# Perceiver block on one core: the output projection of the cross-attention moved around the key sums, the value product behind the next scores, 32 columns streamed in the sums, and the first pair's steps in another order

## The chip, the core and the metric

The kernel runs on one NeuronCore of a Trainium2 chip. Its engines are TensorE (PE, matmuls; its weight loads are shown apart as PEld), VectorE (DVE), ScalarE (ACT), GpSimd (POOL) and SyncE (SP), which issues nearly all DMAs here. Each engine takes its own list of instructions in order and waits on semaphores. The metric is the time of one execution on the device in microseconds (us); lower is better.

## The reference

A block of three parts, each added to x (512 tokens of 512 values, kept in fp32). In short:

```
x = x + cross_attention(layernorm(x), ctx)   # 8 batches: 64 queries, 256 keys; 16 heads of 128
x = x + chunked_linear_attention(layernorm(x))
x = x + moe(layernorm(x))                    # 32 experts, top 6, and a shared one

# cross_attention, per head h
q = rmsnorm(x @ Wq[h]) * gq ;  k = rmsnorm(ctx @ Wk[h]) * gk ;  v = ctx @ Wv[h]
out += softmax(q @ k.T / sqrt(128)) @ v @ Wo[h]
```

The change lies in the cross-attention alone.

## The kernel before

**Precision.** Most products are made of three passes on operands split into a high and a low part (`mm3`, lines 319 to 321): ACT copies the high part, DVE or POOL subtracts it to get the low part, and PE runs high x high, high x low, low x high. The sums of squares, the scores and the product with the probabilities are plain fp32.

**Pairs of heads.** The cross-attention takes heads two at a time, in HP = 8 pairs. `pair(0)` is written out, pairs 1 to 6 are the bodies of a hardware loop (`Fori`), and `last_pair` is written out again. A pair i works one stage ahead: while it makes its own softmax, it projects queries and keys for pair i+1, and it projects the output of pair i-1 (called y in the code) to x. On PE a body of the loop is: scores of pair i in four parts (`xa_pe_scores`, L724, two batches a part), queries of pair i+1 (`xa_pe_q`), its keys in eight parts (`xa_pe_keys`), the sums of squares of its keys and queries (`xa_pe_ss`, L707 and L711), the output projection of pair i-1 in four tiles of 128 tokens (`xo_pe`, `xo_pe_tile`), a transpose of the reciprocal norms (`xa_pe_rkT`, L717), then for each part the transposes of the probabilities (`xa_pe_pT`, L735) and their product with the context (`xa_pe_u`, L748), and last the product with the value weights (`xa_pe_ao`), which needs all four parts of u split in two.

**The sums.** A sum over the 128 partitions is a matmul with the squares as weights. `xa_pe_ss` loads 32 columns of squares as weights, streams one column of ones through them, and writes one PSUM column on 32 partitions; four such matmuls fill the 128. There are 128 for the keys and 32 for the queries in each pair, and each fp32 matmul stands as two instructions in the trace.

**Who feeds whom.** DVE multiplies scores with the keys' reciprocal norms `rkB` (L639), takes the maximum (L642) and scales it (L644); ACT takes the exponential (L606); DVE normalises (L649, L651). DVE copies the keys out of PSUM (L581), ACT squares them (`xa_act_ksq`, L576). After the sums come ACT's square root (`xa_act_rms`, L656), DVE's reciprocal (`xa_dve_rq`, L660), the transpose on PE, DVE's copy (L585), and on SP a store to DRAM and a broadcast load into `rkB`, for the next pair's scores. `xo_act_heads` and `xo_dve_heads` (L402, L407) split the result of `xa_pe_ao`; both stand at the end of a pair. `xo_dve` adds the four tiles of the projection to x (L444).

**Banks.** PSUM has eight banks of 512 fp32. `SB` gives the banks of the four score parts, `KB` those of the eight key parts, `SSB` that of the sums, `YB` and `YL` those of the projection's tiles. u takes banks 4 and 5, ao 6 and 7, the queries 2 and 3.

**The order** on each engine is the order of the calls in the code; nothing is scheduled. The first pair's keys, the first layer norm (`ln_*`) and the first queries stand ahead of `pair(0)` on every engine.

Of the kernel before, what the change touches and what calls it, by code (L numbers as in the profile page):

```python
# [38 lines left out]
def perceiver_block(nc, x_in, ctx_in, ctxT_in, Wq, Wk, WkT, Wv, Wo, gq, gk,  # L39
# [17 lines left out]
    with stack:  # L57
# [327 lines left out]
        SB = (4, 5, 0, 1)  # L385
# [29 lines left out]
        def xo_pe(e, i, last=False):  # L415

            e.wait_ge(wo_ready, i * 2 + 2)
            e.wait_ge(ao_split, i * 2 + 2)
            for t in range(TT):
                if last and t >= 2:  # L420
                    e.wait_ge(s_ready, (i + 1) * 4 + t + 1)
                if not last and t < 2:
                    e.wait_ge(kT_ready, (i + 2) * NK + (4 + t + 1))
                if not last and t >= 2:
                    e.wait_ge(qn_ready, (i + 2) * 2 + (t - 1))
                xo_pe_tile(i, t, YL[t] if last else YB[t])
# [124 lines left out]
        KB = (6, 7, 4, 5, 0, 1, 6, 7)  # L551
# [101 lines left out]

        def xa_act_rms(e, p):
# [42 lines left out]
        def xa_pe_ss(e, p):  # L697

# [3 lines left out]
            for n in range(NK):  # L702
                for s in range(4):
                    col = B + n % 2 * KT + n // 2 * 4 + s
                    for r in range(4):
                        at = s % 2 * P + r * Q4
                        m = e.matmul(ps[r * Q4:(r + 1) * Q4, SSB, col:col + 1], ksq(n)[:, s // 2, at:at + Q4],  # L707
                                     ones[:, 0:1], start=True, stop=True)
            for b in range(B):
                for r in range(4):  # L710
                    m = e.matmul(ps[r * Q4:(r + 1) * Q4, SSB, b:b + 1],  # L711
                                 sq[:, b, r // 2, r % 2 * Q4:(r % 2 + 1) * Q4], ones[:, 0:1], start=True, stop=True)
            m.then_inc(ss_ps, 1)

        def xa_pe_rkT(e, p, bank):
            e.wait_ge(soft_step, p * SOFT + 1)
# [580 lines left out]
        soft_step, rms_ready = sem("soft_step"), sem("rms_ready")  # L1297
# [238 lines left out]
        def _(e):  # L1536
# [8 lines left out]
            ctxT_hi(0)  # L1545
            ctxT_hi(1)
            for n in range(NK):
                xa_act_ksq(e, 0, n)
                if n in (1, 3):
                    ctxT_hi(2 + n // 2)  # L1550
                if n == 5:
                    ln_act_std(e, 0, 0, TT)
            xa_act_wq(e, 0)
            for t in range(TT):
                ln_tile_hi(e, 0, t)
            e.wait_ge(small_dve, DV_GQK)
# [3 lines left out]
            xa_act_rms(e, 0)  # L1560
            xa_act_wk(e, 1)

            def pair(i, more=True):
                xa_act_exp(e, i, 0)
                xa_act_wv(e, i)
                xa_act_exp(e, i, 1)
# [19 lines left out]
                xo_act_heads(e, i)  # L1586
            pair(0)
            with e.Fori(1, HP - 2) as i:
                pair(i)
            pair(HP - 2, False)  # L1590

            def last_pair(i):
                xa_act_exp(e, i, 0)
                xa_act_wv(e, i)
                for j in range(1, JB):
# [87 lines left out]
        def _(e):  # L1683
# [6 lines left out]
            ctxT_lo(0)  # L1690
            ctxT_lo(1)
            for n in range(NK):
                xa_dve_kT(e, 0, n)
                if n in (1, 3):
                    ctxT_lo(2 + n // 2)
                if n == 2:
                    e.wait_ge(x_in_s, 16)
                if n in (2, 3):
                    for t in range(2):
                        ln_stats(e, 2 * n - 4 + t)  # L1700
                if n == 4:
                    ln_mean_var(e)
            ln_tiles_inverse(e, 0, TT, 1)
            for t in range(TT):
                ln_tile_scale(e, t, xn_a)
            e.wait_ge(g_in_s, 32)
            e.tensor_tensor(gqk[:, 2:3], gqk[:, 0:1], gqk[:, 1:2], ALU.mult).then_inc(small_dve, 1)
            for t in range(TT):
                ln_tile_lo(e, 0, t)
# [518 lines left out]
```

## Time and profile before

| what | value |
|---|---|
| median of 3 runs | 1041.73 us (1037.94 to 1043.43) |
| the profiled execution: its own time, its span | 1042.17 us, 1040.4 us |
| mean granted TensorE clock | 0.962 of full |
| TensorE busy (share of the span) | 965.2 us (93%) |
| VectorE, ScalarE, GpSimd busy | 643.4 us (62%), 569.1 us (55%), 263.5 us (25%) |
| cross-attention | from the start to about 425 us |

The profile's span is the part between the first and the last recorded instruction; 1.8 us of the execution lie outside of it. A timeline row gives start, duration, engine, line, operation, output and inputs, and in square brackets how long the engine had idled before and who released it. A matmul's duration holds its way through the array; the cost of one in a dense row of them is the distance between starts. Consecutive instructions of one line are merged into a row with a count. "issue" as a releaser means that the profile shows nothing that was waited for.

### The profile page before, as it was taken

What the parts mean: (1) busy time and instruction counts of PE and PEld (TensorE: products, weight loads), DVE (VectorE), ACT (ScalarE), POOL (GpSimd) and SP (SyncE); (2) the same over time, 40 slices, a digit from 0 to 9 for tenths busy, and PEclk for the clock granted to TensorE, in tenths of its full rate; (3) what the DMA queues carried; (4) which work ended last, traced back from release to release, by engine and by line L of the source; (5) the groups of instructions that cost most, each with busy time, mean ns of one, the idle gap of its engine ahead of it and who ended that gap; (6) DMA issues with size and microseconds to landing.
All of it is one profiled execution on the core that took longest, in us unless ns stands there. A gap on an engine that the chain in (4) does not pass through costs nothing.

```text
span 1040.4 us, 23883 instructions
## 1 busy us (share of the span) xinstructions
PE 965.2 (93%) x8410; PEld 804.8 (77%) x8411; DVE 643.4 (62%) x1009; ACT 569.1 (55%) x925; POOL 263.5 (25%) x167
## 2 busy tenths in 40 slices
PE   7677889999999989989999999899999999999997
PEld 5556677777778778778888888777878889878885
DVE  5252535445352627667777777574848888778876
ACT  4353536446363637455555563444247888778773
POOL 0202202111111104133333330010023544545451
PEclk9897998989898989999999999999999999999999
DMA  4342320303031113422222200711348999998995
GB/s 161 113 113 72 133 72 30 91 10 102 3 99 33 39 41 84 152 82 81 81 81 81 71 30 25 246 40 41 117 161 291 283 318 323 361 340 273 308 347 173
DMA packets 74884, 143.07 MB, mean 138 GB/s; under 512 B 13556, under 2 KB 40564, under 8 KB 74592
## 3 DMA queue, kind: packets, MB, share of 16 engines
q1 hardware_dynamic: 66992, 130.43, 37.1%
q0 software_dynamic: 7856, 12.16, 5.1%
q8 instruction: 23, 0.38, 0.2%
q14 instruction: 13, 0.11, 0.0%
HBM read 144.76 MB, written 15.07 MB: 154 GB/s over the span
## 4 chain that ended last, share of the span: by engine, by line
PE 71%; DMA 8%; DVE 6%; SPq 5%; issue 5%; ACT 4%; DVEq 0%; ACTq 0%; POOLq 0%
PE ps L319 17%; PE ps L320 16%; PE ps L321 16%; PE ps L748 6%; PE ps L724 3%; DMA w_raw<-in_w 3%; SPq L1001 2%; PE ps L707 2%; PE ps L1034 2%; DMA wo_raw<-in_owT 1%; DMA y_scratch<-ob,give 1%; DMA w_and_lists<-in_w 1%; PE ps L1046 1%; SPq L1242 1%; PE ps L735 1%
## 5 line engine op out<-in xcount | busy, mean ns | idle before, releaser
L1059 DVE TENSOR_TENSOR w_l<-w_raw,w_h 128x1408 fp32r<-128x1408 f32 x76 | 121.8, 1624 | 32.7 <-ACT w_h L1055 24.9
L1055 ACT ACTIVATE w_h<-w_raw 128x1408 fp32r (+1 forms) x76 | 102.9, 1376 | 35.4 <-DMA w_raw<-in_w 32.9
L778 POOL TENSOR_TENSOR lw_l<-lw_raw,lw_h 128x1024 fp32r<-128x1024 f32 x32 | 77.3, 2432 | 133.8 <-ACT lw_h L774 128.9
L319 PE MATMUL ps<-w_h,xeT_h 128*128 128x352 f32 x288 | 97.4, 338 | 5.5 <-DVE w_l L1059 5.0
L320 PE MATMUL ps<-w_l,xeT_h 128*128 128x352 f32 x288 | 93.1, 323 | 0.0
L321 PE MATMUL ps<-w_h,xeT_l 128*128 128x352 f32 x288 | 92.9, 323 | 0.0
L1215 POOL DMA_INDIRECT xe<-xn_scratch,take x37 | 39.5, 1069 | 183.3 <-DVE give L1163 100.5
L1219 POOL DMA_INDIRECT y_scratch<-ob,give x34 | 80.2, 2357 | 22.5 <-issue 9.9
L319 PE MATMUL ps<-xT_hi,lw_h 128*128 128x512 f32 x192 | 78.2, 407 | 0.3
L321 PE MATMUL ps<-xT_hi,lw_l 128*128 128x512 f32 x192 | 76.4, 398 | 0.0
L320 PE MATMUL ps<-xT_lo,lw_h 128*128 128x512 f32 x192 | 76.1, 397 | 0.0
L748 PE MATMUL ps<-pT,ctx 128*128 128x128 f32 x512 | 63.7, 281 | 1.7 <-ACT pT L612 1.7
L581 DVE COPY kT<-ps 128x512 f32<-128x512 f32 x64 | 43.5, 688 | 33.1 <-PE ps L321 33.1
L748 PEld LDWEIGHTS ps<-pT,ctx 128*128 128x128 f32 x512 | 60.7, 196 | 3.6 <-ACT pT L612 3.6
L319 PEld LDWEIGHTS ps<-w_h,xeT_h 128*128 128x128 f32 x288 | 54.3, 189 | 10.1 <-DVE w_l L1059 10.1
L319 PE MATMUL ps<-cT_h,wk_h 128*128 128x512 f32 x128 | 51.9, 406 | 8.7 <-DVE cT_l L1687 5.1
L319 PE MATMUL ps<-wo_h,ao_h 128*128 128x512 f32 x128 | 57.0, 446 | 3.0 <-DVE ao_l L483 2.6
L397 POOL TENSOR_TENSOR wo_l<-wo_raw,wo_h 128x512 fp32r<-128x512 f32 x16 | 20.3, 1289 | 153.2 <-ACT wo_h L392 153.2
L665 DVE TENSOR_TENSOR u_l<-ps,u_h 128x512 fp32r<-128x512 f32 x32 | 22.1, 692 | 57.5 <-ACT u_h L617 57.5
L937 DVE RECIPROCAL q_r<-q_r 128x512 f32<-128x512 f32 x16 | 53.6, 3348 | 6.1 <-ACT q_r L913 6.1
L320 PE MATMUL ps<-wo_l,ao_h 128*128 128x512 f32 x128 | 54.8, 428 | 0.0
L321 PE MATMUL ps<-wo_h,ao_l 128*128 128x512 f32 x128 | 54.2, 423 | 0.0
(315 smaller groups left out, 2522.4 us busy)
## 6 DMA issues: line engine op xcount, KB each, us to landing
w_raw<-in_w SPq DMA_DIRECT2D x78, 704.0 KB
w_and_lists<-in_w SPq DMA_DIRECT2D x39, 512.0 KB
w_and_lists<-in_w SPq DMA_DIRECT2D x39, 192.0 KB
rkB<-rk_scratch SPq DMA_DIRECT2D x56, 128.0 KB, 3.1
wq_raw<-in_Wq SPq DMA_DIRECT2D x8, 512.0 KB, 5.1
wo_raw<-in_Wo SPq DMA_DIRECT2D x16, 256.0 KB, 2.7
lw_raw<-in_kwT SPq DMA_DIRECT2D x8, 512.0 KB, 3.3
lw_raw<-in_qwT SPq DMA_DIRECT2D x8, 512.0 KB, 3.4
```

What stands on the lines that cost most here:

```text
L319: nc.tensor.matmul(out_ap, lh, rh, start=first, stop=False)
L320: nc.tensor.matmul(out_ap, lh, rl, start=False, stop=False)
L321: return nc.tensor.matmul(out_ap, ll, rh, start=False, stop=last)
L581: e.tensor_copy(kT[:, n % 2, n // 2 * G4:(n // 2 + 1) * G4], ps[:, KB[n], :]).then_inc(kT_ready, 1)
L724: m = e.matmul(ps[k * SQ:(k + 1) * SQ, SB[j], n * SKV:(n + 1) * SKV], qn[:, k, b * SQ:(b + 1) * SQ], kT[:, k, kvb(b)], start=True, stop=True)
L748: m = e.matmul(ps[:, 4 + j % 2, at:at + P], ctx[:, b * KPB + t, hcol(c)], pT[:, b, t, :], start=t == 0, stop=t == KPB - 1)
L778: e.tensor_tensor(lw_l[n][:, :, :], lw_raw[n][:, :, :], lw_h[n][:, :, :], ALU.subtract).then_inc(lw_ready[n], 1)
L937: e.reciprocal(q_r[:, k, :], q_r[:, k, :]).then_inc(q_recip, 1)
L1055: e.activation(w13_h[:, k, n, :, :], w13_raw[:, slot(raw), n, :, :], ACT.Copy).then_inc(w13_hi_s, 1)
L1059: e.tensor_tensor(w13_l[:, k, n, :, :], w13_raw[:, slot(raw), n, :, :], w13_h[:, k, n, :, :], ALU.subtract).then_inc(w13_ready, 1)
L1215: e.indirect_dma_start(xe[:, k, :], None, xn_dram.ap(), bass.IndirectOffsetOnAxis(ap=take[:, k:k + 1], axis=0), bounds_check=T - 1, oob_is ...
L1219: e.indirect_dma_start(y_dram[k].ap(), bass.IndirectOffsetOnAxis(ap=give[:, k:k + 1], axis=0), ob[:, k, :], None, bounds_check=T - 1, oob_ ...
```

## The change

Seven edits, all within the cross-attention:

- `xo_pe` in the loop is split (`xo_pe_half`): tiles 0 and 1 now stand ahead of the sums, tiles 2 and 3 behind them. Tiles 0 and 1 wait for two of the key copies instead of for later ones. On DVE the additions of tiles 0 and 1 stand ahead of the reciprocal, and the others behind it.
- `xa_pe_ao` of pair i-1 stands in pair i, behind its four scores (in the last pair behind three of them). The splits `xo_act_heads` and `xo_dve_heads` go with it: on ACT behind the second exponential, on DVE behind the fourth scores. The copy of the value weights on ACT waits until ao has been made.
- The banks of scores are 0, 1, 4, 5 and those of key parts 2 to 5 are 0, 1, 4, 5, so that the first two scores don't touch u's banks. Scores 2 and 3 wait for the last two parts of u.
- The sums stream 32 columns of ones instead of one. Each matmul writes 32 PSUM columns, and the next of its rows overwrites all but the first; the queries' sums are made ahead of the keys', in order of columns.
- Ahead of pair 0 the keys' sums are made before the queries, and the queries' sums by themselves later, with their own square roots and reciprocals (`xa_act_first_rms`, `xa_dve_first_rk`, `xa_act_first_rms_q`, `xa_dve_first_rq`). The transpose of the keys' norms stands between the two query products.
- Ahead of pair 0, ACT makes all four high parts of the context before it squares keys, DVE three of the low parts before it copies keys; the copies, statistics and weight splits around them are reordered.
- The warm-up matmuls at the very start are 21 instead of 16.

```diff
-        SB = (4, 5, 0, 1)
+        SB = (0, 1, 4, 5)
-        KB = (6, 7, 4, 5, 0, 1, 6, 7)
+        KB = (6, 7, 0, 1, 4, 5, 6, 7)
...
+        def xo_pe_half(e, i, half):
+
+            e.wait_ge(wo_ready, i * 2 + 2)
+            e.wait_ge(ao_split, i * 2 + 2)
+            for t in (2 * half, 2 * half + 1):
+                if t < 2:
+                    e.wait_ge(kT_ready, (i + 2) * NK + (2 + t + 1))
+                else:
                     e.wait_ge(qn_ready, (i + 2) * 2 + (t - 1))
-                xo_pe_tile(i, t, YL[t] if last else YB[t])
+                xo_pe_tile(i, t, YB[t])
...
         def xa_act_wv(e, i):
             e.wait_ge(wv_in, i * 16 + 16)
+            if not isinstance(i, int) or i > 0:
+                e.wait_ge(ao_ps, i * 2)
...
+        def xa_pe_k_ss(e, p):
+            for k in range(2):
+                for t in range(KT):
+                    col = B + k * KT + t
                     for r in range(4):
-                        m = e.matmul(ps[r * Q4:(r + 1) * Q4, SSB, col:col + 1], ksq(n)[:, s // 2, at:at + Q4],
-                                     ones[:, 0:1], start=True, stop=True)
+                        at = t % 2 * P + r * Q4
+                        m = e.matmul(ps[r * Q4:(r + 1) * Q4, SSB, col:col + Q4], ksq(t // 4 * 2 + k)[:, t % 4 // 2, at:at + Q4],
+                                     ones[:, 0:Q4], start=True, stop=True)
...
         def xa_pe_u(e, i, j):
             e.wait_ge(pT_ready, i * 4 + (j + 1))
             if j < 2:
-                e.wait_ge(s_ready, i * 4 + (j + 1))
+                e.wait_ge(s_ready, i * 4 + (j + 3))
...
@@ ACT, pair @@
                 xa_act_exp(e, i, 0)
+                xa_act_exp(e, i, 1)
+                if y is not None:
+                    xo_act_heads(e, y)
                 xa_act_wv(e, i)
-                xa_act_exp(e, i, 1)
...
@@ DVE, pair @@
                 xa_dve_scores(e, i, 3)
+                if y is not None:
+                    xo_dve_heads(e, y)
                 xa_dve_norm(e, i, 2)
...
+                if y is not None:
+                    xo_dve_tile(e, y, 0, YB)
+                    xo_dve_tile(e, y, 1, YB)
                 xa_dve_rq(e, i + 1)
                 if y is not None:
-                    xo_dve(e, y)
+                    xo_dve_tile(e, y, 2, YB)
+                    xo_dve_tile(e, y, 3, YB)
...
@@ PE, ahead of pair 0 @@
+            e.wait_ge(kT_ready, NK)
+            e.wait_ge(ksq_ready, NK)
+            xa_pe_k_ss(e, 0).then_inc(first_ss, 1)
             e.wait_ge(xT_ready, TT)
             xa_pe_q(e, 0, 0)
+            xa_pe_rkT(e, 0, 6)
             xa_pe_q(e, 0, 1)
-            xa_pe_ss(e, 0)
+            e.wait_ge(sq_ready, 2)
+            xa_pe_q_ss(e).then_inc(ss_ps, 1)
@@ PE, pair @@
+                    if j >= 2 and y is not None:
+                        e.wait_ge(u_ready, y * 4 + (j + 1))
                     xa_pe_scores(e, i, j)
-                if isinstance(i, int) and i == 0:
-                    xa_pe_rkT(e, 0, 6)
+                if y is not None:
+                    xa_pe_ao(e, y)
                 xa_pe_q(e, i + 1, 0)
                 xa_pe_q(e, i + 1, 1)
                 xa_pe_keys(e, i)
+                if y is not None:
+                    xo_pe_half(e, y, 0)
                 xa_pe_ss(e, i + 1)
                 if y is not None:
-                    xo_pe(e, y)
+                    xo_pe_half(e, y, 1)
...
-                xa_pe_ao(e, i)
@@ PE, last pair @@
                 for j in range(JB):
+                    if j >= 2:
+                        e.wait_ge(u_ready, (i - 1) * 4 + (j + 1))
                     xa_pe_scores(e, i, j)
+                    if j == 2:
+                        e.wait_ge(u_ready, (i - 1) * 4 + 4)
+                        xa_pe_ao(e, i - 1)
                 xo_pe(e, i - 1, last=True)
```

**PE, the loop, at its seam.** The end of the loop's body before: transposes of the probabilities, their product with the context (L748), ao (`u_h,wv_h`), the jump back.

```order
L735 MATMUL ps<-ident,sc 128x128 x4
L748 MATMUL ps<-pT,ctx 128x128 x16
L319 MATMUL ps<-u_h,wv_h 128x512
L320 MATMUL ps<-u_l,wv_h 128x512
L321 MATMUL ps<-u_h,wv_l 128x512
```

And the start of the body in the changed kernel (L758 is the scores' line there, was L724; L2079 sets up the waits for u's splits), the end of which is now the product with the context:

```order
L758 MATMUL ps<-kT,qn 64x256 x8
L2079 ISA
L758 MATMUL ps<-kT,qn 64x256 x4
L2079 REGISTER_ALU
L758 MATMUL ps<-kT,qn 64x256 x4
L319 MATMUL ps<-u_h,wv_h 128x512
L320 MATMUL ps<-u_l,wv_h 128x512
L321 MATMUL ps<-u_h,wv_l 128x512
```

The twelve matmuls of ao have moved over the seam, behind the sixteen of the next scores, with the waits for u between the scores.

**PE, the loop, around the sums.** Before: the sums (weights from `lw_raw`, `ksq` and `sq`) follow on the last key part, and the projection (`wo_h,ao_h`) on them.

```order
L699 ISA
L700 REGISTER_ALU
L707 MATMUL ps<-ones,lw_raw 32x1 x16
L707 MATMUL ps<-ones,ksq 32x1 x16
L707 MATMUL ps<-ones,lw_raw 32x1 x16
L707 MATMUL ps<-ones,ksq 32x1 x16
L707 MATMUL ps<-ones,lw_raw 32x1 x16
L707 MATMUL ps<-ones,ksq 32x1 x16
L707 MATMUL ps<-ones,lw_raw 32x1 x16
L707 MATMUL ps<-ones,ksq 32x1 x16
L711 MATMUL ps<-ones,sq 32x1 x32
```

In the changed kernel, with the last rows of tile 1 ahead and the first of tile 2 behind:

```order
L320 MATMUL ps<-wo_l,ao_h 128x512
L321 MATMUL ps<-wo_h,ao_l 128x512
L723 ISA
L724 REGISTER_ALU
L742 MATMUL ps<-ones,sq 32x32 x32
L735 MATMUL ps<-ones,lw_raw 32x32 x64
L735 MATMUL ps<-ones,ksq 32x32 x64
L432 REGISTER_ALU
L319 MATMUL ps<-wo_h,ao_h 128x512
```

The count of sums is the same, 160; each streams 32 columns, and half the projection stands on either side.

**DVE, the loop, behind the fourth scores.** In the changed kernel the split of ao (L407) stands between the scaled maximum (L653, was L644) and the third normalisation; before, these rows stood at the end of the body.

```order
L653 TENSOR_TENSOR nmx<-nmx,rqk 128x2
L406 ISA
L407 TENSOR_TENSOR ao_l<-ps,ao_h 128x512
L406 REGISTER_ALU
L407 TENSOR_TENSOR ao_l<-ps,ao_h 128x512
L658 RECIPROCAL rsm<-sm 128x2
```

The first scores of a pair have nothing of ao ahead of them now; keys' parts 0 and 1, which reuse ao's banks, wait for these two rows.

## Rows read from the trace of the kernel before

**Rows 1.** Waits of PE from 0 to 400 us: total, times, longest.

```profile
PE ps L707 <- ACT ksq L576: 11.9, 7, 2.7
PE ps L319 <- DVE u_l L665: 10.5, 7, 1.5
PE ps L707 <- issue: 5.8, 3, 2.3
PE ps L319 <- DVE cT_l L1687: 5.1, 3, 2.2
PE ps L319 <- DVE xT_lo L374: 4.0, 1, 4.0
PE ps L711 <- issue: 3.4, 2, 1.9
PE ps L319 <- DVE sc L639: 3.2, 4, 1.6
```

**Rows 2.** Timeline of PE, pair 2, from its scores to the next pair's.

```profile
152.98 3.67 PE L724 MATMUL ps<-kT,qn 128*64 128x256 f32 x32
...
173.01 0.39 PE L320 MATMUL ps<-cT_l,wk_h 128*128 128x512 f32 x1
173.25 0.40 PE L321 MATMUL ps<-cT_h,wk_l 128*128 128x512 f32 x1
175.18 0.40 PE L707 MATMUL ps<-ones,lw_raw 128*32 128x1 f32 x29 [1.54 <-ACT ksq L576]
...
178.99 0.79 PE L319 MATMUL ps<-wo_h,ao_h 128*128 128x512 f32 x1
...
182.99 0.40 PE L319 MATMUL ps<-wo_h,ao_h 128*128 128x512 f32 x1
...
197.59 0.47 PE L319 MATMUL ps<-u_h,wv_h 128*128 128x512 f32 x1 [1.50 <-DVE u_l L665]
...
200.53 3.67 PE L724 MATMUL ps<-kT,qn 128*64 128x256 f32 x32
```

**Rows 3.** Windows: busy time of each engine, then granted clock, DMA share, GB/s.

```profile
177.00:179.00 2.00, 2.00 (x155) 1.99 (x147) 0.00 (x0) 0.80 (x1) 2.00 (x2) 0.50 0.00 0
183.00:185.00 2.00, 2.00 (x10) 1.67 (x9) 0.69 (x1) 0.00 (x0) 0.00 (x0) 1.00 0.00 0
```

**Rows 4.** Timeline of PE: sums before pair 0, and in pair 2.

```profile
40.89 0.43 PE L707 MATMUL ps<-ones,lw_raw 128*32 128x1 f32 x32 [0.69 <-ACT sq L593]
41.16 0.42 PE L707 MATMUL ps<-ones,ksq 128*32 128x1 f32 x31
...
177.16 0.60 PE L707 MATMUL ps<-ones,lw_raw 128*32 128x1 f32 x30
...
177.59 0.60 PE L707 MATMUL ps<-ones,ksq 128*32 128x1 f32 x30
```

**Rows 5.** Timeline of PE, second layer: 64 columns streamed, then one.

```profile
445.20 1.15 PE L817 MATMUL ps<-kq 128*64 128x64 f32 x32
446.18 1.05 PE L807 MATMUL ps<-ones,kq_sq 128*64 128x1 f32 x32
447.16 0.50 PE L319 MATMUL ps<-xT_hi,lw_h 128*128 128x512 f32 x1
```

**Rows 6.** Timeline of PE, pair 0: scores, sums and their end.

```profile
47.10 5.01 PE L724 MATMUL ps<-kT,qn 128*64 128x256 f32 x32 [0.39 <-ACT rms L656]
...
76.62 0.40 PE L707 MATMUL ps<-ones,lw_raw 128*32 128x1 f32 x29 [2.68 <-ACT ksq L576]
...
84.33 0.28 PE L711 MATMUL ps<-ones,sq 128*32 128x1 f32 x7 [1.85 <-issue]
```

**Rows 7.** Timeline of DVE, last pair: first scores, last scaled maximum.

```profile
392.42 0.68 DVE L639 TENSOR_TENSOR sc<-ps,rkB 128x512 f32<-128x512 f32 x1
...
400.03 0.16 DVE L644 TENSOR_TENSOR nmx<-nmx,rqk 128x2 f32<-128x2 f32 x1
```

**Rows 8.** Timeline of PE, last pair: its first transposes.

```profile
400.83 1.04 PE L735 MATMUL ps<-ident,sc 128*128 128x128 f32 x8
```

More of the change, by code:

```diff
@@ L420, in xo_pe @@
                 if last and t >= 2:
[L421 to L424, printed above, removed]
+                    e.wait_ge(s_ready, (i + 1) * 4 + t - 1)
+                xo_pe_tile(i, t, YL[t] if last else YB[t])
+        def xo_pe_half(e, i, half):
[5 more added lines that the diff above has]
+                else:
                     e.wait_ge(qn_ready, (i + 2) * 2 + (t - 1))
-                xo_pe_tile(i, t, YL[t] if last else YB[t])
+                xo_pe_tile(i, t, YB[t])
         def ao_half(n):
@@ L1544, in _ @@
             xa_act_wk(e, 0)
-            ctxT_hi(0)
-            ctxT_hi(1)
-            for n in range(NK):
+            for g in range(4):
+                ctxT_hi(g)
+            for n in range(4):
                 xa_act_ksq(e, 0, n)
[L1549 to L1552, printed above, removed]
             xa_act_wq(e, 0)
-            for t in range(TT):
+            for n in range(4, 6):
+                xa_act_ksq(e, 0, n)
+            ln_act_std(e, 0, 0, TT)
+            xa_act_ksq(e, 0, 6)
+            ln_tile_hi(e, 0, 0)
+            xa_act_ksq(e, 0, 7)
+            for t in range(1, TT):
                 ln_tile_hi(e, 0, t)
+            xa_act_first_rms(e)
+            xa_act_wk(e, 1)
             e.wait_ge(small_dve, DV_GQK)
@@ L1585, in pair @@
                 xo_act_weights(e, i)
-                xo_act_heads(e, i)
             pair(0)
             with e.Fori(1, HP - 2) as i:
-                pair(i)
-            pair(HP - 2, False)
+                pair(i, y=i - 1)
+            pair(HP - 2, False, HP - 3)
             def last_pair(i):
                 xa_act_exp(e, i, 0)
+                xa_act_exp(e, i, 1)
+                xo_act_heads(e, i - 1)
                 xa_act_wv(e, i)
-                for j in range(1, JB):
+                for j in range(2, JB):
                     xa_act_exp(e, i, j)
@@ L1689, in _ @@
             xa_wk_low(e, 0)
-            ctxT_lo(0)
-            ctxT_lo(1)
-            for n in range(NK):
-                xa_dve_kT(e, 0, n)
[L1694 to L1702, printed above, removed]
+            for g in range(3):
+                ctxT_lo(g)
+            xa_dve_kT(e, 0, 0)
+            xa_dve_kT(e, 0, 1)
+            ctxT_lo(3)
+            xa_dve_kT(e, 0, 2)
+            xa_dve_kT(e, 0, 3)
+            e.wait_ge(x_in_s, 16)
+            for t in range(TT):
+                ln_stats(e, t)
+            ln_mean_var(e)
+            for n in range(4, 7):
+                xa_dve_kT(e, 0, n)
             ln_tiles_inverse(e, 0, TT, 1)
@@ L1751, in last_pair @@
                 xa_dve_scores(e, i, 3)
+                xo_dve_heads(e, i - 1)
                 xa_dve_norm(e, i, 2)
@@ L2000, in _ @@
             e.wait_ge(consts, 2)
-            for _ in range(16):
+            for _ in range(21):
                 e.matmul(ps[:, 0, 0:P], ones[:, :], ones[:, :], start=True, stop=True)
```

50 lines of the change are left out of this document (33 added, 17 removed).

## The prediction

> **What bounds the kernel now.** I read the busy shares first: TensorE is busy 93% of the span, no other engine over 62%, so TensorE's list of work sets the time, and a gain must come from its idle stretches, from a higher clock, or from less work. The second view is the list of TensorE's waits up to 400 us, where the cross-attention lies [rows 1]. The reader is to see three kinds: 11.9 us for the squared keys ahead of the sums (7 times), 10.5 us for u's low part ahead of ao (7 times, 1.5 us each), and 9.2 us (5.8 and 3.4) of "issue" inside the sums, in five pieces, one of them in rows 6. Third, one pair of the loop in the timeline [rows 2]: it takes 200.53 - 152.98 = 47.55 us, and shows the two waits (1.54 and 1.50) and a stretch of projection matmuls that start 4.00 us apart for nine of them, where the keys' start 0.24 us apart. Fourth, the granted clock of windows [rows 3]: 0.50 of full in the sums and behind them (1.2 GHz), 1.00 (2.4 GHz) from 183 us. The engine's history before that fall is an idle stretch of 1.5 us and then matmuls that stream one column each. So a pair loses about 5 us that are not work, and the sums are slower than they could be.
>
> **The steady pair, term by term.** The change puts half the projection, 12 matmuls or 2.8 us, between the last keys and the sums. ACT's last square comes 1.5 us behind the keys, so the wait goes: the last key matmul starts at 173.25 and would be followed 0.24 later, the sums start at 175.18, so 1.69 us [rows 2]. Cover: 2.8 against 1.5 us. Behind the sums stand the other 12 matmuls, 2.8 us; square root, reciprocal and their hand-overs need about 1 us there, and were covered by all four tiles before. Ao, moved behind the next scores, has 16 scores (3.6 us) as cover for u's last split, whose wait is 1.50 us [rows 2]. Cover again suffices, and the waits for u in the scores ask for it only after 1.8 and 2.7 us of scores. That is 1.50 more.
>
> The sums: 320 instructions (160 fp32 matmuls of two each) took 178.99 - 175.18 = 3.81 us [rows 2]. At full clock 32 start within 0.27 us, at half clock within 0.43 [rows 4], so all of them at full clock would be 2.7. What 32 streamed columns cost no row shows. The nearest rows from either side are in the second layer [rows 5]: 32 instructions with 64 weight columns that stream 64 columns take 446.18 - 445.20 = 0.98 us, and 32 with the same weights and one column 447.16 - 446.18 = 0.98 too. Equal times say that the stream lies wholly beside the weight load. On that side the sums cost 2.7 us as with one column; on the other side each costs what a streaming instruction of that row costs, 31 ns, and 320 of them 9.8 us. I take 2.7: the streamed columns and the weight columns are both halved against that row, and one column against 64 made no difference there. No lower end than 2.7 is to be had, since loads stay. So the sums give 3.81 - 2.7 = 1.1 us.
>
> If the clock stays up, the nine slow matmuls cost 9 x 0.24 = 2.2 instead of 4.0 us: 1.8. I take it that it does: nothing idles ahead of the sums any more, and the sums keep the array streaming. The changed pair is 1.7 + 1.5 + 1.1 + 1.8 = 6.1 us shorter, 41.4 us; six bodies give 37 us. The stalls on issue in the first body stay.
>
> **What could come in its place.** The splits of ao now wait on ACT behind two exponentials, on DVE behind four scores. DVE's chain from first scores to last scaled maximum takes 400.03 + 0.16 - 392.42 = 7.8 us [rows 7]; it starts some 1.4 us into the scores, and two splits of the size of its multiplication there, 0.68, follow, so they are done 10.6 us into the pair. The keys that want the banks start after scores 3.6, ao 200.53 - 197.59 = 2.9 [rows 2] and queries 24 x 0.24 = 5.7, at 12.2 us: 1.6 us to spare. Queued behind the waiting split on ACT are the copy of the value weights, which POOL and then SP's next load of them wait for, and the third exponential; the weights are wanted a whole pair later. SP's order is unchanged, and its store and loads of the norms start at the same distance behind the sums. I cost these edits at nothing.
>
> **The last pair** does lose. Its projection stands right behind the scores, and now has ao's splits ahead of it, which DVE makes after all four scores: 10.6 us into the pair, then 24 matmuls, 5.6, so the transposes start at 16.2. Before, wait and ao (1.5 + 2.9), scores 3.6 and projection until the transposes at 400.83 [rows 8], some 6.2, make 14.2. Loss 2.0 us, bounds 0 and 4 (by whether DVE starts its chain at once).
>
> **The first pair.** (a) The sums and what follows took 47.10 - 40.89 = 6.2 us ahead of the first scores [rows 4, 6]; 64 of 320 instructions remain, 0.5: gain 5.7. The other 256 move into the wait of 4.0 us for the tokens' low part [rows 1]; at half clock they are 3.4 us, and may bring their stall on issue of 2.3: I cost that at nothing, against a gain of 1 from the 5.1 us for the context's low parts [rows 1], since key copies and statistics on DVE stay in one line with it. (b) Scores at 5.01 instead of 3.67 [rows 2, 6], for a low clock: 1.3. (c) The waits for scores, 3.2 [rows 1]: with the transpose of the norms ahead of the second query product, the norms land before the scores are there: 3.2. (d) The wait for squares is 2.68, a DVE that is late; 1.5 stays: 1.2. (e) The sums take 84.33 - 76.62, with the last few 7.8 us, of which 3.5 are stalls that stay; 2.7 + 3.5 = 6.2: 1.6. Together 14 us; bounds 6 (the 256 sums and their stall uncovered, the clock low) and 20 (the context's waits gone whole). More warm-up matmuls end ahead of the first keys and cost nothing.
>
> **Sum.** 14 + 37 - 2 = 49 us. The profiled execution took 1042.2, 0.4 over the median; 1042.2 - 49 = 993 us, about 993 against the median too. The layers behind only shift.
>
> The Trainium skill speaks against the price of the sums: by "TensorE: Matmul & The Clock Gate" (section "Wait — 56ns, not 53.3ns?") starts of matmuls never come closer than about 25 ns, however few columns they stream. Rows 4 disagree: 32 instructions in 0.27 us are 8 ns each, on four groups of 32 array columns in turn.
>
> **The rivals.**
> - The clock falls in the sums as before. For it: they remain short loads on a quarter of the array; against: no idle stretch ahead, and more columns. It gives back the 1.1 and 1.8 us of the pair, six times, and some 2 us in pair 0: 993 + 20 = 1013.
> - A wait in the place of the removed ones: the 1.6 us to spare for the keys' banks go, by exponentials that ACT makes late behind ao. For it: both engines' queues now hold a wait for ao in the softmax chain; against: the sum above. At 2 us in each of six bodies: 1005.
> - The first pair gives only its lower bound of 6: 1001. For it: the stalls on issue have no cause in the profile.
> - Slower: the streams do not overlap, and a sums instruction costs 31 ns [rows 5]. For it: this is the only measured price of an fp32 instruction that streams tens of columns to a part of the array; against: its weight loads alone explain it, as the one-column rows cost the same. Sums 9.8 instead of 2.7, eight times (start, pair 0, six bodies): 57 us, 1050. It decides from 28 ns on (49 / 8 = 6.1 us more per set, 8.8 in all); above that the change loses.
> - A floor per instruction that only streaming ones meet, between the 8 ns of rows 4 and the 31 ns of rows 5: at 24 ns, 320 cost 7.8 us, 5.1 more, eight times: 1034. The page's figure of 25 ns would be this case (8.0 us, 1035 as an estimate), and rows 4 leave little for it.
>
> **How the numbers follow.** Forecast 0.60 (985 to 1000), clock 0.12, new wait 0.12, first pair 0.06, overlap missing 0.07, floor 0.03. The range of 8 in 10 goes from 984, where the first pair gives 20 and the pair's terms a little more, to 1013, which takes in the clock's case and leaves about 1 in 10 above. A difference of 0.5% (5 us) is what a measurement of this kernel can tell from none. Faster by more: 0.92; within: 0.01; slower: 0.07.
>
> **What the changed profile would show.** Distance between two pairs' scores 41 to 42 us. No wait for u's low part and none for squares in the loop. Granted clock 1.00 in the sums, which take about 2.7 us; the projection's matmuls 0.24 us apart on both sides. First scores of pair 0 near 39 us, and no wait for scores in its keys. A new wait of about 4 us for ao's split in the last pair. The forecast is wrong if the sums last over 5 us at full clock, if the window behind them shows 0.50, or if the keys wait for ao's split.

## The result: 38 us faster, 11 short of the forecast

| | before | after |
|---|---|---|
| median (range) of 4 runs each | 1042.58 us (1037.94 to 1044.28) | 1004.66 us (1002.77 to 1006.04) |
| ratio, 95% interval | | 0.9642 [0.9605, 0.9678] |
| profiled execution, its span | 1042.17, 1040.4 us | 1006.04, 1004.3 us |
| mean granted TensorE clock | 0.962 | 0.977 |

The forecast was 993 us. The time lies within the range (984 to 1013), above the likeliest case's own (985 to 1000).

The page of the changed kernel, busy time of each engine:

```profile
PE 951.0 (95%) x8420; PEld 797.7 (79%) x8421; DVE 646.9 (64%) x1010; ACT 569.3 (57%) x926; POOL 263.7 (26%) x167
```

TensorE is still the bound, with 14 us less of busy time; the other 22 us of the shorter span are idle time that has gone. Its waits up to 400 us (total, times, longest), to hold against [rows 1]:

```profile
PE ps L735 <- issue: 12.8, 6, 3.6
PE ps L357 <- DVE xn_a L349: 4.8, 1, 4.8
PE ps L319 <- DVE ao_l L407: 4.6, 1, 4.6
PE ps L782 <- ACT pT L621: 1.7, 7, 0.3
PE ps L742 <- ACT ksq L583: 1.5, 1, 1.5
```

The 11.9 us for squares are down to 1.5 in pair 0, and the 10.5 us for u's low part, the 4.0 for the tokens and the 3.2 for scores are gone. The one new wait of the forecast is there: 4.6 us for ao's split (L407), once. A second one, not forecast, has grown: the transposes of the first layer norm (L357) wait 4.8 us for DVE, where they waited 1.5. What the forecast had wrong stands in the first line: the stalls on issue in the sums (L735) have grown from 9.2 us [rows 1] to 12.8.

One body of the loop in the timeline of PE, changed kernel, to hold against [rows 2] (start, duration, engine, line, operation):

```profile
138.75 3.67 PE L758 MATMUL ps<-kT,qn 128*64 128x256 f32 x32
...
164.85 0.73 PE L742 MATMUL ps<-ones,sq 128*32 128x32 f32 x62
...
165.43 1.23 PE L735 MATMUL ps<-ones,lw_raw 128*32 128x32 f32 x125
...
166.50 1.25 PE L735 MATMUL ps<-ones,ksq 128*32 128x32 f32 x126
167.69 0.49 PE L319 MATMUL ps<-wo_h,ao_h 128*128 128x512 f32 x1
168.02 0.39 PE L320 MATMUL ps<-wo_l,ao_h 128*128 128x512 f32 x1
168.25 0.40 PE L321 MATMUL ps<-wo_h,ao_l 128*128 128x512 f32 x1
...
180.15 3.67 PE L758 MATMUL ps<-kT,qn 128*64 128x256 f32 x32
```

The body takes 41.40 us, and so do the next four (41.38 to 41.40); 41.4 was forecast. The 320 sums take 167.69 - 164.85 = 2.84 us, 8.9 ns each; 2.7 was forecast. The window of the sums, to hold against [rows 3] (its granted clock is the third number from the end, then DMA share and GB/s):

```profile
164.00:168.00 4.00, 4.00 (x326) 3.49 (x325) 0.95 (x2) 2.52 (x4) 3.42 (x2) 1.00 0.00 0
```

The clock is 1.00 (2.4 GHz) there, and the projection's matmuls behind are 0.23 us apart (168.02 to 168.25, and so on).

Where the rest went shows at the start. Timeline of PE, changed kernel, ahead of pair 0:

```profile
25.38 3.65 PE L357 MATMUL ps<-ident,xn_a 128*128 128x128 f32 x16 [4.79 <-DVE xn_a L349]
28.96 1.57 PE L735 MATMUL ps<-ones,lw_raw 128*32 128x32 f32 x114
34.16 0.39 PE L735 MATMUL ps<-ones,lw_raw 128*32 128x32 f32 x12 [3.63 <-issue]
...
34.36 1.73 PE L735 MATMUL ps<-ones,ksq 128*32 128x32 f32 x112
37.90 0.44 PE L735 MATMUL ps<-ones,ksq 128*32 128x32 f32 x14 [1.80 <-issue]
38.26 0.80 PE L319 MATMUL ps<-xT_hi,wq_h 128*128 128x512 f32 x1
...
47.34 0.76 PE L742 MATMUL ps<-ones,sq 128*32 128x32 f32 x64 [0.69 <-ACT sq L602]
48.03 3.67 PE L758 MATMUL ps<-kT,qn 128*64 128x256 f32 x32
```

And DVE, which makes the tokens' low part that the queries wait for:

```profile
29.69 0.69 DVE L374 TENSOR_TENSOR xT_lo<-ps,xT_hi 128x512 fp32r<-128x512 f32 x1 [0.16 <-ACT xT_hi L368]
```

The tokens are ready at 30.4 us, but the queries start at 38.26, because the 256 sums in front stall twice, for 3.63 and 1.80 us. In the kernel before, the queries started as soon as the tokens came. The same place in its PE timeline:

```profile
32.83 0.79 PE L319 MATMUL ps<-xT_hi,wq_h 128*128 128x512 f32 x1 [3.97 <-DVE xT_lo L374]
```

So the queries start 5.4 us later than before. From there to the first scores it is 9.8 us instead of 14.3, so the first scores stand at 48.03 us; before they stood at 47.10 [rows 6], and 39 was forecast.

The last pair, timeline of PE of the changed kernel, and the window behind its wait:

```profile
345.73 2.81 PE L758 MATMUL ps<-kT,qn 128*64 128x256 f32 x24
...
357.07 0.47 PE L319 MATMUL ps<-wo_h,ao_h 128*128 128x512 f32 x1 [4.56 <-DVE ao_l L407]
...
364.22 1.03 PE L769 MATMUL ps<-ident,sc 128*128 128x128 f32 x8
```

```profile
357.00:361.00 4.00, 3.93 (x11) 3.13 (x12) 2.15 (x4) 0.03 (x1) 0.00 (x0) 0.58 0.66 5
```

From scores to transposes it is 18.5 us where 14.2 were counted before.

**The ledger**, by starts on PE (the stretches end where PE begins to wait for u's low part before, and with the scores after):

| stretch | before | after | gained | forecast |
|---|---|---|---|---|
| start to pair 0's scores | 47.10 | 48.03 | -0.9 | 6.7 (a) |
| pair 0 | 50.2 | 42.8 | 7.4 | 7.3 (b to e) |
| first body of the loop | 51.2 | 47.9 | 3.3 | 6.1 |
| five more bodies | 238.1 | 207.0 | 31.1 | 30.5 |
| last pair until the transposes | 14.2 | 18.5 | -4.3 | -2 |
| sum | | | 36.6 | 49 |

The spans differ by 36.1.

### The profile page after: what moved, and what is told of

Its sections match the earlier page's. It is cut to its first block, busy times and chain, and to the rows that moved or that the text cites. A ratio compares the mean times of both kernels' runs of the same rounds, so it can differ in the third digit from the quotient of the medians.

```text
span 1004.3 us, 23929 instructions
## 1 busy us (share of the span) xinstructions
PE 951.0 (95%) x8420; PEld 797.7 (79%) x8421; DVE 646.9 (64%) x1010; ACT 569.3 (57%) x926; POOL 263.7 (26%) x167
## 4 chain that ended last, share of the span: by engine, by line
PE 74%; DMA 8%; SPq 6%; issue 5%; DVE 5%; ACT 3%; DVEq 0%; ACTq 0%; POOLq 0%
PE ps L319 18%; PE ps L321 17%; PE ps L320 17%; PE ps L782 6%; PE ps L758 3%; DMA w_raw<-in_w 3%; SPq L1035 2%; PE ps L735 2%; PE ps L1068 2%; DMA y_scratch<-ob,give 2%; DMA w_and_lists<-in_w 1%; PE ps L1080 1%; PE ps L769 1%; SPq L1276 1%; DMA wo_raw<-in_owT 1%
## 5 line engine op out<-in xcount | busy, mean ns | idle before, releaser
L1089 ACT ACTIVATE w_h<-w_raw 128x1408 fp32r (+1 forms) x76 | 102.7, 1375 | 31.5 <-DMA w_raw<-in_w 29.1
L1253 POOL DMA_INDIRECT y_scratch<-ob,give x34 | 82.5, 2426 | 21.8 <-issue 9.1
L319 PE MATMUL ps<-wo_h,ao_h 128*128 128x512 f32 x128 | 53.4, 417 | 6.9 <-DVE ao_l L407 4.6
L631 POOL TENSOR_TENSOR wq_l<-wq_raw,wq_h 128x1024 fp32r<-128x1024 f32 x8 | 19.1, 2385 | 136.8 <-ACT wq_h L572 136.8
L320 PEld LDWEIGHTS ps<-w_l,xeT_h 128*128 128x128 f32 x288 | 54.2, 188 | 0.0
L321 PEld LDWEIGHTS ps<-w_h,xeT_l 128*128 128x128 f32 x288 | 54.1, 188 | 0.0
```

What stands on the lines that cost most here:

```text
L319: nc.tensor.matmul(out_ap, lh, rh, start=first, stop=False)
L320: nc.tensor.matmul(out_ap, lh, rl, start=False, stop=False)
L321: return nc.tensor.matmul(out_ap, ll, rh, start=False, stop=last)
L1089: e.activation(w13_h[:, k, n, :, :], w13_raw[:, slot(raw), n, :, :], ACT.Copy).then_inc(w13_hi_s, 1)
L1253: e.indirect_dma_start(y_dram[k].ap(), bass.IndirectOffsetOnAxis(ap=give[:, k:k + 1], axis=0), ob[:, k, :], None, bounds_check=T - 1, oob_ ...
```

## The experiments

Three questions: what holds the clock and how much each part of the pair's change is worth (e1, e5, e6, e9); why the start gained nothing (e2, e3, e7); and what the last pair's wait costs (e4, e8, e10). Each ratio is to the kernel before on the same chip.

**e1, one column.** The changed kernel, with one column streamed in every sum.

```diff
-  m = e.matmul(ps[..., col:col + Q4], ksq(...)[...], ones[:, 0:Q4], ...)
+  m = e.matmul(ps[..., col:col + 1], ksq(...)[...], ones[:, 0:1], ...)
```

> The changed kernel with one column streamed in the sums instead of 32; all else stays. Theory A (the clock falls where the sums stream one column, whatever stands around them): in the loop the granted clock falls to 0.5 in or behind the sums, and the second half of the projection starts its matmuls 0.43 us apart; a body takes 43 to 44.5 us instead of 41.4, the kernel 1004.7 + 6 x 2 to 3 = 1017 to 1023 us. Rival B (the fall came from the idle 1.5 us ahead of the sums, which the split has taken away, and the 32 columns do nothing): a body stays at 41.2 to 41.5 us with the clock at 1.00, the kernel at 1003 to 1006 us, a little less if a streamed column costs anything.

Median 1006.6 us (1002.91 to 1008.29), ratio 0.9659 [0.9603, 0.9715], against 0.9642 for the changed kernel: no difference that can be told, and close to rival B. In the second body the sums take 166.78 - 163.97 = 2.81 us where 32 columns took 2.84. The Trainium skill has this as a rule in "TensorEngine Tiling (Array Packing)", section Instruction Overhead (a matmul over one column takes as long as one over 60); the trace agrees, with 2.81 and 2.84. The first body of the loop takes 47.59 us, with its stalls; of the five others four take 41.38 at full clock, and one 42.95, where the clock falls behind the sums (window; granted clock third from the end):

```profile
292.00:294.00 2.00, 2.00 (x6) 1.53 (x5) 0.69 (x1) 0.00 (x0) 0.00 (x0) 0.50 0.00 0
```

So with no idle stretch ahead one column keeps the clock up in most bodies, not in all, and the columns are worth about 2 us here by the medians, which lies inside the spread of either kernel's runs.

**e5, the columns alone.** The kernel before, with 32 columns and, as in the diff of the change, the queries' sums ahead of the keys' in order of columns (a sum's extra columns have to be overwritten by the next). Nothing else.

> The kernel before with the sums streaming 32 columns, and nothing else of the change. Theory B (the idle 1.5 us ahead of the sums and the one-column sums together let the clock fall; without a gap it mostly stays, as the one-column run of the changed kernel showed): with 32 columns behind the gap the clock may stay too, since more of the array's time is in use; then each of six bodies gains 1.1 + 1.8 = 2.9 us and the kernel 17 us, 1024 us. Rival C (32 columns change nothing and the gap alone decides): the clock falls as before, a body stays at 47.5 us, the kernel at 1038 to 1043 us.

1024.82 us (1023.09 to 1026.29), ratio 0.9851 [0.9812, 0.989]. The body is 240.71 - 195.85 = 44.86 us. PE timeline and the windows around it:

```profile
218.05 0.72 PE L704 MATMUL ps<-ones,sq 128*32 128x32 f32 x62 [1.54 <-ACT ksq L576]
...
220.99 0.49 PE L319 MATMUL ps<-wo_h,ao_h 128*128 128x512 f32 x1
```

```profile
218.00:221.00 3.00, 2.90 (x321) 2.82 (x321) 0.00 (x0) 2.68 (x4) 2.07 (x1) 1.00 0.00 0
221.00:225.00 4.00, 4.00 (x18) 3.29 (x19) 1.78 (x3) 0.27 (x1) 1.56 (x2) 1.00 0.00 0
```

The wait of 1.54 us is still there, and the clock stays at 1.00 in and behind the sums. Against [rows 3], where one column after the same wait ran at 0.50, the columns by themselves hold the clock: from 151 to 375 us, which takes in the five later bodies, its mean is 1.00. The order of the sums changed with them and was not tried alone.

**e6, the split alone.** The kernel before, with the projection's two halves around the sums of one column (on DVE its additions likewise).

```diff
+                if y is not None:
+                    xo_pe_half(e, y, 0)
                 xa_pe_ss(e, i + 1)
-                    xo_pe(e, y)
+                    xo_pe_half(e, y, 1)
```

> The kernel before with its projection split around the sums on PE and DVE, one column, and nothing else of the change. The wait for the squares (1.7 us a body) goes in any case: 10 us in six bodies. Theory B (no gap, mostly no fall): the slow projection and the slow sums go too in most bodies, another 2.9 us each: a body takes 42.9 us and the kernel 1042 - 25 to 28 = 1014 to 1017 us. Rival A (one-column sums drop the clock by themselves): a body takes 45 to 46 us, the kernel 1029 to 1033 us.

1023.58 us (1020.82 to 1027.09), ratio 0.9846 [0.98, 0.9891]. The wait for squares is gone from the loop, but the clock falls a little later. Windows, sums first:

```profile
176.00:178.00 2.00, 2.00 (x262) 2.00 (x254) 0.58 (x1) 1.28 (x1) 2.00 (x2) 1.00 0.00 0
178.00:180.00 2.00, 2.00 (x81) 1.67 (x72) 0.40 (x1) 0.29 (x1) 1.15 (x1) 0.81 0.00 0
180.00:182.00 2.00, 2.00 (x6) 1.62 (x5) 0.69 (x1) 0.00 (x0) 0.00 (x0) 0.50 0.00 0
```

Behind the first body (50.08 us, with its stalls) come four of 44.6 to 44.7 us and one of 43.12. The run lies between the two expectations: an idle stretch ahead isn't needed for the fall, and without one it comes later or, in one of five bodies here and four of five in e1, not at all. It falls late in the sums or behind them, and stays low about half as long as before. e6 keeps the wait of 1.5 us for u's low part in each body, which e1 doesn't have; whether that or something else makes the clock fall in more bodies here stays open.

**e9, split and columns.** Both edits on the kernel before; ao's place and the start as they were.

> The kernel before with the projection split and the 32 columns, but ao, the banks and the start as they were. If ao's move is worth its wait of 1.5 us a body and nothing else, a body takes 41.4 + 1.5 = 42.9 us here, with the clock at 1.00 throughout, and the kernel 1015 to 1019 us. Rival (one of the two, columns or split, makes the other's gain void): a body of 44.7 to 44.9 us as with either alone, 1023 to 1025 us.

1015.86 us (1013.91 to 1018.58), ratio 0.9742 [0.9706, 0.9778]. The body is 194.04 - 150.89 = 43.15 us, full clock throughout, and u's waits stay as they were:

```profile
PE ps L319 <- DVE u_l L675: 10.5, 7, 1.5
```

So the body's 6.2 us come as 4.4 from the two edits together, and 43.15 - 41.40 = 1.75 from ao's place. Alone, the columns save 2.7, which is the slow stretch, and the split 2.9, which is the wait of 1.7 and a part of the same slow stretch; that part counts once.

**e2, wide sums at the start.** Ahead of and in pair 0 each sum has 128 columns of squares as weights instead of four times 32, so that 80 instructions do for 320. The loop stays.

```diff
+                    if isinstance(p, int) and p < 2:
+                        m = e.matmul(ps[:, SSB, col:col + Q4], ksq(...)[..., t % 2 * P:(t % 2 + 1) * P], ones[:, 0:Q4], ...)
+                        continue
```

> The changed kernel; the sums ahead of pair 0 and in pair 0 (not in the loop) load all 128 columns of squares at once, 40 matmuls a set (80 instructions) instead of 160 (320); 32 columns are streamed as before, and the sums come out the same. Theory A (each stall on issue is a refill of TensorE's instructions from memory, which comes due per 256 instructions and shows where many short ones are drained at once): the two stalls ahead of pair 0 (5.4 us) and the two in it (3.9 us) shrink to 0 to 3 us together, against 1 to 3 us that the wider loads cost; the kernel takes 997 to 1002 us. Rival B (the stalls belong to the sums themselves, to matmuls on parts of the array or to their time): they stay at 8 to 9 us and the wider loads come on top, 1004 to 1008 us.

1014.85 us (1012.86 to 1015.18), ratio 0.9751 [0.9699, 0.9804]: 10 us slower than the changed kernel. Its stalls on issue, and the start in the PE timeline:

```profile
PE ps L739 <- issue: 3.5, 2, 2.2
```

```profile
28.57 3.77 PE L734 MATMUL ps<-ones,lw_raw 128*128 128x32 f32 x32
32.15 7.02 PE L734 MATMUL ps<-ones,ksq 128*128 128x32 f32 x32
```

The four stalls ahead of and in pair 0 are gone, only the loop's own 3.5 us are left. Packets on the instruction queue still come (one from 28 to 40 us, one from 64 to 86 us), but PE no longer waits. The edit makes the instructions fewer and slower at once and uses the whole array, so it shows that the stalls need many short instructions, not whether their number, their pace or their shape counts. But 32 wide ones take 3.58 us at a granted clock of 0.98 (112 ns each) and 7.02 at 0.50 (219 ns), and that is more than the stalls were. The time lies above both expectations: my price for a full-width load (1 to 3 us in all) was wrong.

**e3, the big loads later.** The changed kernel; SP issues the loads of the context (2 MB) and of the value weights behind the first load of the norms.

```diff
-            e.dma_start(wv_raw[:, :, :], wv_r[0]).then_inc(wv_in, 16)
-            e.dma_start(ctx[:, :, :], ctx_in.rearrange("(t p) c -> p t c", p=P)).then_inc(ctx_in_s, 16)
...
+            e.dma_start(wv_raw[:, :, :], wv_r[0]).then_inc(wv_in, 16)
+            e.dma_start(ctx[:, :, :], ctx_in.rearrange("(t p) c -> p t c", p=P)).then_inc(ctx_in_s, 16)
```

> The changed kernel; the first load of the value weights (256 KB) and the load of the context (2 MB) stand behind the first load of the norms instead of ahead of it. Theory A (the first refill, 3.6 us against about 2 elsewhere, is late because it queues behind these loads): the first stall falls to about 2 us, and if the clock gets up sooner for it the first queries too; the kernel takes 1001 to 1004 us. Rival B (it is long for another cause, such as the clock): 3.6 us stays, 1004 to 1006 us. A third way: the late loads of 2.3 MB push back the first norms or weights, and the time rises over 1006.

999.3 us (996.41 to 1001.55), ratio 0.9598 [0.9542, 0.9655]. PE timeline of its start:

```profile
30.84 0.29 PE L735 MATMUL ps<-ones,lw_raw 128*32 128x32 f32 x12 [1.00 <-issue]
...
34.58 0.33 PE L735 MATMUL ps<-ones,ksq 128*32 128x32 f32 x14 [2.45 <-issue]
34.84 0.50 PE L319 MATMUL ps<-xT_hi,wq_h 128*128 128x512 f32 x1
...
43.73 3.67 PE L758 MATMUL ps<-kT,qn 128*64 128x256 f32 x32
```

What the DMA queues did in those stretches, first the changed kernel from 28 to 40 us, then e3 from 28 to 34 us (packets, MB, share of 16 engines):

```profile
q1 hardware_dynamic: 1726, 1.75, 43.6%
q8 instruction: 3, 0.05, 1.7%
```

```profile
q8 instruction: 2, 0.03, 2.7%
```

An "instruction" packet of about 16 KB comes with each stall, and in shorter windows of the same view each stall ends 2.2 to 3.1 us after its packet starts. In the changed kernel the first starts between 31.5 and 32.0 us, amid the two big loads and some 3 us after the sums began; the first stall is 3.63 us and ends at 34.16. In e3 it starts between 28.0 and 28.5, as the sums begin; the stall is 1.00 us and ends at 30.84. Other runs agree: with the loads in place the first stall is 3.92 (e1) and 2.01 (e4), with them moved 0.76 (e8), and in e10, where a packet starts between 26.0 and 26.5, about 3 us ahead of the sums (29.46), there is none. The next stall is 2.45 instead of 1.80, though nothing else is loading: a stall isn't cured by this, the long one is cut. First scores stand 4.3 us sooner. Of these, 2.0 are the two stalls (3.45 against 5.43), and the rest goes with the clock, which is low for less time ahead of the scores: 0.50 throughout from 34 to 42 us in the changed kernel, and only around 36 to 39 us here. The median lies below both expectations. The medians were not taken side by side, and the intervals overlap, so the trace carries this, not the ratio.

**e7, the old start.** The changed kernel with the order of before ahead of and around pair 0 on PE, ACT and DVE; the loop and the last pair stay changed.

> The changed kernel with what stands ahead of pair 0 put back as it was (all sums behind the queries, the norms' transpose in pair 0, the old order of context splits, key copies and statistics). Theory A (the new start gives little, since its 256 sums pay two refills of instructions where one was paid before, at a low clock): it loses what the norms' early landing gives in pair 0 (3.2 + 1.2 us) and gains or loses 1 to 3 at the start; 1005 to 1010 us. Rival B (the new start gives the 14 us that were forecast for it): 1017 to 1020 us.

1008.75 us (1005.55 to 1011.31), ratio 0.9708 [0.967, 0.9746]. Pair 0's scores start at 46.25 and the loop at 95.14; in the changed kernel at 48.03 and 90.86. The new start loses 1.8 us ahead of the scores and gives 6.1 in pair 0: 4.3 up to the loop, of the 14 forecast. The old start's stalls (8.4 us in five) are the shorter ones. In the first body, whose code is the same in both, e7 then wins back 3.1 us: it takes 139.96 - 95.14 = 44.82 us instead of 47.89, and 1.2 us of the 4.3 are left when the second body starts. The window behind the stalls there, first the changed kernel, then e7:

```profile
124.00:128.00 4.00, 4.00 (x13) 3.14 (x11) 1.09 (x2) 0.29 (x1) 0.00 (x0) 0.50 0.01 4
```

```profile
124.00:128.00 4.00, 1.82 (x136) 1.61 (x123) 0.11 (x1) 0.29 (x1) 0.59 (x1) 1.00 0.01 4
```

So in e7 the clock doesn't fall in the first body. What decides it isn't shown; its stalls there are 0.6 us shorter in sum (0.79 and 2.18 against 1.06 and 2.46). Up to the last pair's scores (346.99 and 345.73) the profiles give the new start 1.3 us, and the profiled spans are 1003.8 and 1004.3. The medians differ by 4.1. So its worth at the end is 4 us at most, and may be about 1.

**e4, earlier splits in the last pair.** The changed kernel; DVE splits ao behind the third scores there.

```diff
+                xo_dve_heads(e, i - 1)
                 xa_dve_scores(e, i, 3)
-                xo_dve_heads(e, i - 1)
```

> The changed kernel; in the last pair alone DVE splits ao behind its third scores instead of behind the fourth. If the wait of 4.6 us ahead of the last pair's projection is DVE's order alone, it falls to about 2 us, and the low clock behind it (0.58 for 4 us) may go too: 2 to 4.5 us less, 1000 to 1003 us. Rival: the fourth scores, now later, make the probabilities late for the transposes, and the wait only moves there: 1003 to 1006 us.

997.91 us (997.31 to 998.45), ratio 0.9587 [0.9535, 0.9639]. PE's wait, and the window behind it:

```profile
352.35 0.47 PE L319 MATMUL ps<-wo_h,ao_h 128*128 128x512 f32 x1 [2.25 <-DVE ao_l L407]
```

```profile
352.00:356.00 4.00, 3.65 (x16) 3.07 (x17) 3.58 (x8) 1.70 (x6) 0.85 (x1) 1.00 0.99 174
```

The wait is 2.3 us shorter, and the clock stays up where it fell to 0.58 before, so scores to transposes are 357.90 - 343.33 = 14.6 us instead of 18.5. That is 3.9 us. Other runs agree: behind the wait of 4.6 us the clock falls in the changed kernel, e1, e2, e3 and e7, and behind one of 2.3 us or less in none of e4, e8 and e10. The profiled spans differ by 8.2 us, and not all of it is the edit's: pair 0's scores stood at 46.02 instead of 48.03, in code that is the same, since the first stall was 2.01 us there. So a stall's length varies from run to run by more than 1 us. Another 1.9 us are gained behind the transposes, in code that is the same as well. The median lies below the expected 1000 to 1003.

**e8, both.** The edits of e3 and e4 together.

> The changed kernel with both edits that were faster: the loads of the value weights and the context behind the first norms, and ao's splits in the last pair behind the third scores. They lie 300 us apart, so they add up if each is real: 5 and 4 us less than 1004.7, 994 to 997 us. Rival (each was chip noise of the first pair's refills): 998 to 1004 us.

996.92 us (996.54 to 997.8), ratio 0.9585 [0.9549, 0.962]. Scores at 43.60, the last pair's wait 2.3 us: both effects are there, but the median gains less than the two alone did (7.7 against 5.4 and 6.7), which would fit with the shorter first stall of e4's profiled run; whether e4's other runs had it too isn't shown.

**e10, ao behind two scores in the last pair.** The edit of e3, and in the last pair ao behind the second scores, its splits on ACT behind the first exponential and on DVE ahead of the fourth scores as in e4.

```diff
                 xa_act_exp(e, i, 0)
-                xa_act_exp(e, i, 1)
                 xo_act_heads(e, i - 1)
+                xa_act_exp(e, i, 1)
...
-                    if j == 2:
+                    if j == 1:
```

> The changed kernel with the late loads, and in the last pair ao behind two of the scores instead of three, its splits behind the first exponential on ACT and the first normalisation on DVE. If the wait ahead of the last projection is the distance of ao's split on DVE, it falls to about 1 us or less and the kernel gains 1 to 2 us on the run with both edits: 995 to 996.5 us. Rival (the softmax chain, now 1.4 us later, holds up the transposes): 997 to 999 us.

991.5 us (988.81 to 994.09), ratio 0.9523 [0.9488, 0.9557]: the fastest version by its median, below both expectations, and its interval lies below that of the changed kernel (0.9605 to 0.9678). The last pair in its PE timeline:

```profile
340.13 1.95 PE L758 MATMUL ps<-kT,qn 128*64 128x256 f32 x16
...
347.65 0.47 PE L319 MATMUL ps<-wo_h,ao_h 128*128 128x512 f32 x1 [0.74 <-DVE ao_l L407]
...
353.19 1.03 PE L769 MATMUL ps<-ident,sc 128*128 128x128 f32 x8
```

The wait is down to 0.74 us and the stretch to 13.1, less than the 14.2 of before. Its transposes start 3.1 us sooner than e8's (356.30), yet its span is 9.1 shorter. Part of the rest is in later windows, where e8's clock is lower, e8 first (the same stretches of time, not quite the same work):

```profile
400.00:420.00 20.00, 17.81 (x183) 14.31 (x184) 15.06 (x17) 10.74 (x16) 9.59 (x4) 0.91 0.33 107
620.00:660.00 40.00, 35.45 (x156) 29.07 (x156) 27.71 (x43) 18.63 (x30) 3.00 (x11) 0.96 0.30 87
```

```profile
400.00:420.00 20.00, 17.82 (x137) 14.02 (x135) 13.77 (x19) 9.45 (x13) 8.19 (x4) 1.00 0.33 106
620.00:660.00 40.00, 35.92 (x175) 28.77 (x174) 26.32 (x43) 20.80 (x34) 3.00 (x11) 1.00 0.22 66
```

I did not test why; whether the shift of the later layers does it or chance stays open.

## Why the prediction was right, and where it was wrong

- **The steady pair** was right in each term: 41.40 us, no wait for squares, none for u, sums 2.84 us at full clock. e9 shows ao's share, 1.75 us where 1.5 was forecast.
- **The price of a streamed column**, the largest risk (31 ns or 24 ns against 8), was right: 8.9 ns (e1: 8.8 with one column). The figure of about 25 ns that the Trainium skill gives in "TensorE: Matmul & The Clock Gate" (section "Wait — 56ns, not 53.3ns?") doesn't hold on four groups of array columns in turn.
- **The reason for the clock** was half right. I gave two, no idle stretch ahead and more columns streamed. The columns suffice alone (e5), the missing idle stretch doesn't (e6), and with one column and no idle stretch the clock holds in four of five bodies (e1).
- **ACT's and DVE's queues** hid the moved splits in the loop, as forecast: the keys never wait for ao's split there.
- **Pair 0** was right in its sum (7.4 of 7.3), not in its parts. Scores run 3.67 us and no wait for scores is left; from scores to sums 6.2 us are gained instead of 4.5, since a fourth wait, for the keys' copy, went as well. The sums gain nothing instead of 1.6: their two stalls are 2.19 and 1.66 us (3.5 forecast, in sum), and behind the first the clock falls as it did before (0.50 from 76 to 84 us).
- **The failed step is (a)**: "The other 256 move into the wait of 4.0 us for the tokens' low part [rows 1]; at half clock they are 3.4 us, and may bring their stall on issue of 2.3: I cost that at nothing". The wait they moved into was no longer there. The last key matmul starts at 20.2 us, before at 24.7, but the idle time this opened lies ahead of the transposes (4.8 us instead of 1.5), where the sums don't stand; behind them the tokens are ready at 30.4 us, 1.4 us after the sums begin. And the sums brought two stalls, not one, of 5.4 us. 6.7 were forecast, -0.9 came. Two fit with the count: from one stall to the next PE runs 126 sums here and 128 in pair 0, each with a weight load, about 256 instructions, and 256 sums with their loads are two such blocks. e2 shows that the stalls go when the sums are few and slow instructions, e3 that the first is long when its packet starts late, amid the loads, and e7 that the whole new start gives 4.3 us up to the loop and 1.2 by the second body. The squares of six of the eight key parts are ready at 22.8 us, so a part of the sums could stand in the 4.8 us ahead of the transposes; no run tried that.
- **The first body** gained 3.3, not 6.1. Its stalls stayed as forecast (3.5 us), but behind them the clock falls (0.50 from 124 to 128 us), as it did before. I counted its 1.8 us for the clock all the same. In e7, with shorter stalls, the clock stays at 1.00 and this body gains 6.4 us.
- **The last pair** lost 4.3, not 2.0, just over my bound of 4: DVE made the splits at 11.3 us into the pair instead of 10.6, and behind the idle 4.56 us the clock fell to 0.58 (e4: 3.9 us come back when the wait is halved).
- **The rivals.** "The first pair gives only its lower bound of 6", at 1001, came nearest, with 6.5 measured; I gave it 0.06 although its argument, that the stalls have no cause in the profile, was the one open question of the sum. The number nearest to the result is that of the rival with a new wait, 1005, but by luck: in the loop the keys don't wait for ao's split. The clock's fall in the loop, the missing overlap and the floor did not occur either.

## What to carry to other kernels

Price a dense block that is moved with its own stalls: where code runs for the first time and hundreds of 9 ns instructions follow each other, the refill of instructions is a cost of the block, and it goes along to the new place. Keep big loads out of that stretch. Where a consumer's wait opens in front of a long chain on another engine, as ao's split in the last pair, move the producer earlier (e4, e10), and count the clock that an idle stretch of 4.6 us takes along.

## What the runs showed of the hardware

- **Instruction refills.** In the cross-attention PE stalls on issue only in the sums of code that runs for the first time (the start, pair 0, the first body; none in the five later bodies), for 0.8 to 4.0 us each. A packet of about 16 KB on the instruction queue starts 2.2 to 3.1 us before each of the stalls' ends looked at (changed kernel and e3, the start), and none comes on queue q8 in the changed kernel from 139 to 345 us, in the later bodies (one in e2 and in e3, without a stall). That the packet is what PE waits for is inferred from this timing; the profile names no releaser. The Trainium skill, "Runtime: NRT & Kernel Launch", section Instruction fetch mechanics, says that instructions come in blocks of 16 KiB, 256 instructions, and that the cost of crossing a block is mostly hidden. The block's size agrees with these packets, and the count with the 126 to 128 sums, each with a weight load, between two stalls of the start and of pair 0. The hiding doesn't hold here: at 8.9 ns a sum, 128 sums with their loads last 1.1 us.
- **Weight width.** An fp32 sums instruction with 128 weight columns took 112 ns at a granted clock of 0.98 and 219 at 0.50 (e2), one with 32 columns, on four groups in turn, 8.9 ns. For the same sums that is 112 against 36 ns: small groups in turn are three times as fast.
- **Columns streamed.** 1 and 32 cost the same (2.81 and 2.84 us for 320), and only the 32 keep the clock at 1.00 across an idle stretch of 1.5 us (e5 against [rows 3]).
